# Border of tokenizer and neighbourhood attention: two pairs' deviations spread by TensorE, first keys by head on two engines

## The reference, cut to what matters

```python
h = tok(x)                                     # Fourier features, one hidden layer, gelu, out
h = h + attn0(layernorm(h))                    # neighbourhood attention
h = h + moe(layernorm(h))
h = h + attn1(layernorm(h))
h = h + experts1(layernorm(h))

def layernorm(x, eps=1e-05):
    m = mean(x); v = var(x)
    return (x - m) / sqrt(v + eps)

def attn0(x):                                  # 8 heads of 8, 31 neighbours at dilation 2
    q, k, v = split(x @ w_qkv + b_qkv)
    attn = softmax(q . k[neighbours] / sqrt(8))
    return (attn . v[neighbours]) @ w_proj + b_proj
```

## Time and profile before

| what | us |
|---|---|
| median of 3 executions | 899.4 |
| lowest, highest | 893.36, 900.43 |
| the profiled execution | 896.55 |
| its span, first to last instruction | 894.8 |
| PE busy in the span | 795.4 (89%) |
| DVE, ACT, POOL busy | 576.0, 476.6, 304.9 |

### The profile page before, as it was taken

How to read it: one execution, slowest core, us unless ns; L and a number is a source line. 1 busy time by engine, 2 the same in 40 slices (tenths; PEclk the granted TensorE clock), 3 DMA queues, 4 the chain that set the end, 5 groups by cost and what they waited for, 6 DMA issues and landing times. The chain is left out here.

```text
span 894.8 us, 28767 instructions
## 1 busy us (share of the span) xinstructions
PE 795.4 (89%) x12566; PEld 405.7 (45%) x12566; DVE 576.0 (64%) x849; ACT 476.6 (53%) x656; POOL 304.9 (34%) x296
## 2 busy tenths in 40 slices
PE   4899499999998999758999989799996799999996
PEld 2222177676776766613333223376663233333332
DVE  5537176775775776545877865567673377777776
ACT  2244277776776777536566756422221355555553
POOL 4125553443463352121433455464453620000000
PEclk9889699999999999969999999999998699999998
DMA  4210401001001002010000130053331011111111
GB/s 109 22 28 1 130 28 51 5 4 62 4 4 62 4 5 62 3 60 1 1 2 1 51 92 1 13 167 91 89 94 36 8 30 48 48 49 49 48 49 36
DMA packets 38990, 36.83 MB, mean 41 GB/s; under 512 B 20881, under 2 KB 25138, under 8 KB 38738
## 3 DMA queue, kind: packets, MB, share of 16 engines
q1 hardware_dynamic: 37794, 33.04, 13.2%
q10 hardware_dynamic: 1072, 1.95, 0.7%
HBM read 19.24 MB, written 7.34 MB: 30 GB/s over the span
## 5 line engine op out<-in xcount | busy, mean ns | idle before, releaser
L2043 ACT ACTIVATE se_a<-se_p,cols 128x512 f32<-128x512 f32 x128 | 92.7, 774 | 76.9 <-PE se_p L1996 76.9
L1176 DVE TENSOR_REDUCE na_rowmax<-na_ps 128x16 f32<-128x1024 f32 x64 | 78.0, 1218 | 77.3 <-PE na_ps L1056 77.3
L2063 DVE SCALAR_TENSOR_TENSOR se_a<-se_p,cols,z 128x1024 f32<-128x1024 f32 x64 | 82.2, 1284 | 49.8 <-PE se_p L2006 49.8
L917 POOL TENSOR_TENSOR z<-na_k,const 128x512 f32<-128x512 f32 x64 | 64.6, 1042 | 139.9 <-ACT na_k L1116 139.9
L1418 ACT ACTIVATE z<-me_p,cols 128x512 f32<-128x512 f32 x128 | 81.1, 685 | 55.3 <-PE me_p L1357 50.5
L1550 DVE TENSOR_TENSOR me_gw<-me_pc,z 128x1024 f32<-128x1024 f32 x64 | 78.2, 1222 | 45.2 <-PE me_pc L1369 36.8
L487 POOL TENSOR_TENSOR n_sq<-h 128x512 f32<-128x512 f32 x64 | 68.4, 1074 | 96.2 <-DVE h L839 43.0
L1385 PE MATMUL me_py<-me_gw,w_out 64*64 64x512 f32 x512 | 88.1, 595 | 0.5 <-DVE me_gw L1550 0.5
L1357 PE MATMUL me_p<-z,moe_w 64*64 64x512 f32 x512 | 81.9, 614 | 5.7 <-ACT z L1418 5.7
L522 POOL TENSOR_TENSOR z<-h,n_bc 128x512 f32<-128x512 f32 x60 | 76.3, 1284 | 20.7 <-DMA n_bc<-n_spread 20.7
L1179 DVE TENSOR_TENSOR z<-na_ps,na_rowmax 128x1024 f32<-128x1024 f32 x64 | 78.3, 1224 | 2.2
(11 more groups left out here) (300 smaller groups left out, 1266.0 us busy)
## 6 DMA issues: line engine op xcount, KB each, us to landing
n_bc<-n_spread SPq DMA_DIRECT2D x120, 128.0 KB, 3.0
z<-z SPq DMA_DIRECT2D x64, 128.0 KB, 2.4
out<-se_rows SPq DMA_DIRECT2D x16, 256.0 KB, 2.1
n_spread<-n_rstd SPq DMA_DIRECT2D x12, 256.0 KB, 2.0
const<-in_const ACTq DMA_DIRECT2D x1, 1050.0 KB, 6.9
const<-in_const ACTq DMA_DIRECT2D x1, 562.0 KB, 4.2
f_w<-in_L_ffn_W SPq DMA_DIRECT2D x4, 128.0 KB
const<-in_const ACTq DMA_DIRECT2D x1, 258.0 KB, 3.0
```

What stands on the lines that cost most here:

```text
L1176: nc.vector.tensor_reduce(rowmax[b][:], scored, AX, ALU.max).then_inc(s_max, 1)
L2043: nc.scalar.activation(a1[at.k % 2][:, e2, :], hidden(at.n, e2)[:], ACT.Relu, scale=col(s, "f1_g1", 2 * ep + e2), bias=col(s, "f1_be1", 2 ...
L2063: nc.vector.scalar_tensor_tensor(out=a2[at.k % 2][:], in0=p_2[:], scalar=col(s, "f1_be2", ep), in1=s.f1_w[:, ep, :].unsqueeze(1).broadcast ...
```

## The change

Pairs 0 and 1 (`NEAR` = 2) no longer go through DRAM. A new constant `near_first` has ones that place row 32 p (+ 1) of the deviations on the 64 partitions of each sequence; PE multiplies it with 32 rows of `s.rstd` (`near_of`), and DVE multiplies the result with `h`. For pair 0 that stands at the end of the tokenizer's block, for pair 1 behind the first keys in the attention's block. The first queries go into the PSUM bank of the transposes (`p_first`), and the first even values stand ahead of the first scores. Of the first pair's keys by head, two heads are made on POOL and two on DVE, and on POOL they stand ahead of the multiplications of pairs 2 and 3. SP spreads from pair 2 on.

```diff
+NEAR = 2
...
 def spread_done(stage, p):
-    return 32 * (NP // 4 * stage + p // 4 + 1)
+    return 32 * (NP // 4 * stage + p // 4 + (p % 4 >= NEAR))
+
+def near_of(nc, s, p, bank):
+    rows = slice(32 * p, 32 * p + 32)
+    return nc.tensor.matmul(bank[:], const(s, "near_first")[rows, :], s.rstd[rows, 0, :], start=True, stop=True, skip_group_check=True)
...
             nc.tensor.matmul(p_z[1][:, 0, :], house, s.f1_w1[:].rearrange("p e d -> p (e d)"), start=True, stop=True, skip_group_check=True).then_inc(s_x, 1)
+            te.wait_ge(s.n_rstd, quad(0, LAST))
+            near_of(nc, s, 0, p_m[0]).then_inc(s_near, 1)
             v.tensor_scalar(s.f1_w1[:].rearrange("p e d -> p (e d)"), p_z[1][:, 0, :], kept, None, ALU.mult).then_inc(s_fetched, 1)
+            ve.wait_ge(s_near, 1)
+            v.tensor_tensor(row(s.z, 0), p_m[0][:], row(s.h, 0), ALU.mult).then_inc(s.n_z, 1)
...
+        p_first = p_t[:, 0:4, :].rearrange("p g c -> p (g c)")
...
-                for h in range(HL):
+                for h in range(HL if j > 0 else HL // 2):
...
                     for p in (2 * at.n, 2 * at.n + 1):
-                        pool.wait_ge(s.n_bc[p % 4], spread_done(0, p))
-                        scaled(nc.gpsimd, s, p).then_inc(s.n_z, 1)
+                        if p >= NEAR:
+                            if p == NEAR:
+                                pool.wait_ge(s.n_z, nth(0, NEAR - 1))
+                            pool.wait_ge(s.n_bc[p % 4], spread_done(0, p))
+                            scaled(nc.gpsimd, s, p).then_inc(s.n_z, 1)
...
-            unrolled(NP, 2, (5, before), (0, after), (4, keys_by_head), (0, derive))
+            unrolled(NP, 2, (5, before), (5, first_keys_by_head), (0, after), (4, next_keys_by_head), (0, derive))
...
-            for p in range(NP):
+            for p in range(NEAR, NP):
                 if p >= 4:
                     sp.wait_ge(s.n_z, nth(0, p - 4))
                 spread(sp, s, 0, p, 0)
...
                     nc.tensor.matmul(p_m[:], s.a0_wqk[:, 1, :], row(s.z, j), start=True, stop=True).then_inc(s_k, 1)
+                    if j == 0:
+                        near_of(nc, s, 1, p_o).then_inc(s_near, 1)
...
                     j = at.of(2)
+                    if j == 0:
+                        nc.tensor.matmul(p_first, s.a0_wqk[:, 0, :], row(s.z, j), start=True, stop=True).then_inc(s_q, 1)
+                        return
...
                 te.wait_ge(s_vd, done(at.n - 1))
-                if par == 0:
+                if at.n == 0:
+                    te.wait_ge(s_kd, done(0))
+                elif par == 0:
...
                     te.wait_ge(s_blk, done(j))
+                    if j == 0:
+                        te.wait_ge(s_first, 1)
...
-            unrolled(TURNS, 2, (4, scores), (4, even_values), (6, queries),
+            unrolled(TURNS, 2, (4, scores), (4, even_values), (6, queries), (5, first_values),
...
             give_credits(ve, s_max, s_diff, s_rden, s_on, s_h)
+            ve.wait_ge(s_near, 1)
+            nc.vector.tensor_tensor(row(s.z, 1), p_o[:], row(s.h, 1), ALU.mult).then_inc(s.n_z, 1)
+            ve.wait_ge(s_kd, done(0))
+            for h in range(HL // 2, HL):
+                ins = nc.vector.tensor_tensor(kblk[0][:, h, :, :], kk[0][:], const(s, "headmask")[:, h:h + 1].unsqueeze(2).broadcast_to([128, 2, TG]), ALU.mult)
+            ins.then_inc(s_first, 1)
```

More of the change, by code:

```diff
@@ L58, in window_start @@
     return min(max(t * QT - KW // 2, 0), TG - WIN)
-CONST_PARTS = [("ident", 128), ("dft", 4 * 2 * NF), ("group", 4), ("block", 128), ("cos", T), ("sin", T), ("own", 32), ("place", 60), ("batch", NQ), ("house", 128), ("reflect", D), ("others", 38), ("kept", 1), ("near", 128), ("half_of", 38), ("mean128", 128),
+CONST_PARTS = [("ident", 128), ("dft", 4 * 2 * NF), ("group", 4), ("block", 128), ("cos", T), ("sin", T), ("own", 32), ("place", 60), ("batch", NQ), ("house", 128), ("reflect", D), ("others", 38), ("kept", 1), ("near", 128), ("near_first", 128), ("half_of", 38), ("mean128", 128),
                ("decay", 128), ("chunk_q", 128), ("chunk_k", 1), ("winmask", 4 * WIN), ("headmask", HL), ("vmask", 18), ("rank", NE), ("route_mean", NE),
@@ L82, in constants @@
     c["kept"] = (np.arange(128)[:, None] % D > 0) * 1.0
-    near = np.zeros((4, 32, 2, D))
+    near, near_first = np.zeros((4, 32, 2, D)), np.zeros((4, 32, 2, D))
     for b in range(2):
-        near[:, 2 * LAST + b, b, :] = 1.0
-    c["near"] = near.reshape(128, 128)
+        near[:, 2 * LAST + b, b, :] = near_first[:, b, b, :] = 1.0
+    c["near"], c["near_first"] = near.reshape(128, 128), near_first.reshape(128, 128)
     c["half_of"] = np.zeros((128, 38))
@@ L954, in derive, with first_keys_by_head, next_keys_by_head @@
                     derive_shared(nc, s, step, at.n - 6)
-            unrolled(NP, 2, (5, before), (0, after), (4, keys_by_head), (0, derive))
+            def first_keys_by_head(at):
+                if at.n < 2:
+                    keys_by_head(at)
+            def next_keys_by_head(at):
+                if at.n >= 2:
+                    keys_by_head(at)
+            unrolled(NP, 2, (5, before), (5, first_keys_by_head), (0, after), (4, next_keys_by_head), (0, derive))
         @block.sync
@@ L991, in queries, with first_values @@
                     nc.tensor.matmul(p_m[:], s.a0_wqk[:, 0, :], row(s.z, j), start=True, stop=True).then_inc(s_q, 1)
+            def first_values(at):
+                if at.n == 0:
+                    window_values(at)
             def even_values(at):
-                if at.k == 0:
+                if at.k == 0 and at.n > 0:
                     window_values(at)
@@ L1108, in fetch_queries @@
                     sc.wait_ge(s_score, done(2 * j - 3))
-                    nc.scalar.activation(q[j % 2][:], p_m[:].rearrange("p (t two) -> p two t", two=2), ACT.Identity, bias=col(s, "a0_bq")).then_inc(s_qd, 1)
+                    made = p_m[:] if j > 0 else p_first
+                    nc.scalar.activation(q[j % 2][:], made.rearrange("p (t two) -> p two t", two=2), ACT.Identity, bias=col(s, "a0_bq")).then_inc(s_qd, 1)
             def fetch_keys(at):
@@ L1116, in fetch_keys, with fetch_first_values @@
                     nc.scalar.activation(kk[j % 2][:], p_m[:].rearrange("p (t two) -> p two t", two=2), ACT.Identity, bias=col(s, "a0_bk")).then_inc(s_kd, 1)
+            def fetch_first_values(at):
+                if at.n == 0:
+                    fetch_values(at)
             def fetch_even_values(at):
-                if at.k == 0:
+                if at.k == 0 and at.n > 0:
                     fetch_values(at)
@@ L1163, in deviations @@
                     nc.scalar.activation(s.rstd[:, n, :], s.rstd[:, n, :], ACT.Exp, scale=-0.5).then_inc(s.n_rstd, 1)
-            unrolled(TURNS, 2, (4, fetch_even_values), (6, fetch_queries), (3, fetch(1)), (4, exponential(0)),
+            unrolled(TURNS, 2, (4, fetch_even_values), (6, fetch_queries), (5, fetch_first_values), (3, fetch(1)), (4, exponential(0)),
                      (6, fetch_keys), (4, fetch_odd_values), (4, exponential(1)), (4, fetch(0)), (2, fetch_output), (0, deviations))
```

2 lines of the change are left out of this document (added).

## The result

The changed kernel takes 892.65 us, the median of 20 executions (886.23 to 899.34), against 897.22 of 20 of the kernel before (893.1 to 900.43). The ratio is 0.9954, with a 95% interval of 0.9937 to 0.9972 (it is not the quotient of the two medians, which are 4.6 us apart). A gain of 4.1 us by the ratio is half of the 8.2 us that the forecast summed up. The time lies in its range of 883.5 to 894.5, but that range, 11 us wide, takes in gains of nearly any size; the size of the gain was wrong.

A forecast was written before the change was run, and what follows sets the result against it. PE bounds the attention; the border before it (85 to 110 us) is a chain of waits. DVE's start 7.9 us earlier, 8.25 by the second scores, summed to -8.2 from 896.55: 888.4 us, range 883.5 to 894.5.

The forecast's parts named there:

- the price of product 0: End of the tokenizer: PE spreads pair 0's deviations in 1.12 us at full clock, 90.84 to 91.96.
- the barrier: Between tokenizer and attention: opens at 93.09 instead of 91.55, a cost of 1.54 us on every engine.
- The larger transfer of constants: Start of the kernel: 1114 instead of 1050 KB, some 0.4 us more, counted as hidden before ACT's next block.
- The first step that failed: Behind the barrier: PE makes the first keys in 1.12 us, to 94.2, so ACT's table is late next.
- The second: From 90.35 on: PE hardly idle for more than 1.5 us, so full clock; DVE starts at 101.0, not 108.91.
- All hidden under 99.08: Before the first scores: PE's spread product, queries and values (to about 97.5) end before the keys by head at 99.08.
- the forecast's 7.9: First scores reaching DVE: it starts at 101.0 instead of 108.91, 7.9 us earlier.
- The rival of the clock: Between second keys and transposes: clock falls in a 2.5 us pause, price 3.1 us, time 891.5; chance 0.25.
- The collision of POOL and DVE: First pair's keys by head: the two engines block each other, so 3.46 us instead of 2.08 side by side.
- The rival without collision: First pair's keys by head: side by side in 2.08 us, 1.4 us less, time 887.0; chance 0.13.
- The queue rival: POOL's later pairs delay second or third keys by head; 892.5 with half the gain lost, 895.0 with four fifths; chance 0.08.
- The slower case: Attention's first turns: half clock that doesn't end, slower from about 18 us of it, 900.9 at 25; chance 0.04.

The follow-up runs named there:

- h1: f2 run once more, unaltered, on another chip; ratio 0.9957 to the kernel before.
- g1: f2 with both spread products over all 128 rows of the deviations instead of 32; ratio 0.9928 to the kernel before.
- h2: g1 run once more, on the chip of h1; ratio 0.9926 to the kernel before.
- f3: f2 with PE products of constants: one half-width behind the first spread product, two full behind the second pair's keys; 891.6 us.
- f4: f3 with all four keys by head of the first pair on POOL; its time is not given.
- f2: Changed kernel with PE's eight credit increments and two of ACT's given by POOL; median 893.06 us, ratio 0.9959 to the kernel before.
- g2: f3 with spread products over 128 rows and without ACT's table load at the attention's start; ratio 0.9901 to the kernel before.
- h3: g2 run once more, unaltered; ratio 0.9899 to the kernel before.
- h4: g2 with all four keys by head of the first pair on POOL; median 2.9 us apart from h3's, intervals overlapping.
- e2: Changed kernel with all four keys by head of the first pair on POOL, none on DVE; no difference to the changed kernel.
- g4: Changed kernel with PE's eight credit increments made in two halves each, so sixteen; median 896.36 us against 893.14 for g3.
- e1: Changed kernel with ACT's six credit increments ahead of its table load instead of behind it; its time is not given.
- g3: Changed kernel run once more, unaltered, on the chip of g4; median 893.14 us.
- f1: Changed kernel with PE's eight credit increments given by POOL; ratio 0.9966 to the kernel before.
- e4: e1 with PE products of constants, one behind the first spread product, two behind the second pair's keys; 5.2 us below before.

## Why the prediction was right in its sign and wrong in its size

Right were the start and the price of product 0 (0.05 behind the deviations, 1.12 long), DVE's multiplication from PSUM (0.69) and the barrier (2.18 behind the deviations, forecast 2.31). The larger transfer of constants didn't delay ACT's first block: it begins at 15.16 instead of 15.12. That the border's gain passes to the end was right in the median, as far as it can be told, and not in each execution.

The first step that failed: "PE makes the keys meanwhile (1.12 at full clock, to 94.2). So ACT's table is what is late next, not the keys". The keys did not start at 2.31 but at 3.60 behind the deviations, 1.3 late, because PE works off eight increments of 0.15 first. In the kernel before they lay under the DRAM trip: PE waited 7.65 us there, and the row of its first product showed that wait alone. The forecast costed what the change adds, and not what PE already had standing between the barrier and its first product, once the cover was gone: it put this term at nothing, and it is 1.2 us.

The second: "PE is hardly idle for more than 1.5 us from 90.35 on, so I take full clock". The pause was 2.43 us, of which the first error made 1.2, and the clock fell. The keys (2.04), the spread product (2.07), the queries (2.08) and the values (1.98) then made PE the last at the first scores, where "All hidden under 99.08" had counted 1.6 us of slack. Forecast first scores 8.4 behind the deviations, measured 11.49, so 3.1 us; 0.8 more went in the scores themselves. Together this is the 3.9 us between the forecast's 7.9 and the 4.06 measured at the first maximum.

Of the two steps, the second is the one that the runs tie to the time. It failed also where its premise was met: with pauses of 0.6 to 1.2 us the clock fell in h1, g1, h2, f3 and f4 and held in f2, g2, h3 and h4. And f2 and h1, in which the first error is put right, gained no more in time than the changed kernel. Why the clock falls in one such execution and not in another stays open.

The rival of the clock was named, for the pause behind the second keys. There it came in about half of the profiles, at about the price of 3.1 that the rival had (2.5 between the means). The place one step earlier, with a price of 3.5 us at the first maximum (h1 against f2), it did not have. Its time of 891.5 is nearer to the result than the forecast, by a mechanism of which it had one place of two. A chance of 0.25 was too little.

The collision of POOL and DVE stood as forecast in kind: in the changed kernel DVE's second multiplication took 1.75 instead of 0.69 and ended 0.54 behind POOL's of pair 2, which itself took 1.71:

```profile
99.50 1.71 POOL L529 TENSOR_TENSOR z<-h,n_bc 128x512 f32<-128x512 f32 x1
...
100.00 1.75 DVE L1218 TENSOR_TENSOR z<-na_k,const 128x512 f32<-128x512 f32 x1
```

Its size was 3.03 (in h3) instead of 3.46, and all four on POOL take 4.04, as rows 2 had it, and not the 4.16 of the forecast's upper end (side by side, 95.62 + 2.08 ends at 97.7, not at its 97.6). So the split is worth 1.0 us where the clock holds, and in the changed kernel nothing that was measured (e2), since PE is later. The rival without collision is out. The queue rival is out: pairs 2 and 3 never held the second keys by head, which waited for ACT's fetch in every profile read. The slower case did not come.

## What to carry to other kernels

When a long wait at the start of a block goes away, list everything that the waiting engine still has in its program ahead of that instruction, increments of semaphores included, because all of it was free before. A sum in which one engine has little slack should be made once at each of the two clocks, and for every pause in its chain. And where the clock can fall in a pause, one profile is one draw: it takes many executions to read a median, and the rows of several profiles to read why.

## What the runs showed of the hardware

An increment of a semaphore as an instruction of its own cost PE 0.15 us (g4) and ACT 0.13 (0.79 for six, e1). The eight ahead of the changed kernel's first keys make 1.2 of the 1.3 us by which these were late.

At the first keys the clock was seen to fall behind pauses of 3.7 (g4), 2.4 (changed, g3, e1, e2), 1.8 (f1), 1.7 (e4), 1.2 (h1, g1, h2) and 0.6 us (f3, f4), and to hold once across 1.2 (f2) and three times across 0.8 (g2, h3, h4). At the transposes, one step on, it held five times of ten across 2.6 us. So the length of the last pause alone does not tell, nor did one execution tell what the next would do.

Two multiplications of 128x512 on POOL beside two on DVE take 3.03 us from the first start to the last end (h3), against 4.04 for four on POOL (h4). A table load of the set that is already in place takes ACT 1.28 us like any other (L1135 of the changed kernel); g2 and h3 do without it.
